# One Trainium2 kernel, last stage: another order of the products, scales on GpSimd, and two last groups without casts

## The reference, cut to what matters

```python
y = y.transpose(0, 2, 1, 3).reshape(Bb, Tt, H * HD)
return y @ Wo
...
def _quant_act(x):
    scale = 127.0 / jnp.clip(jnp.max(jnp.abs(x), axis=-1, keepdims=True), EPS, None)
    xq = jnp.clip(jnp.round(x * scale), -128.0, 127.0) / scale
...
h = jax.nn.gelu(_bitlinear(x, w1), approximate=False)
return _bitlinear(h, w2)
...
x = x + _L0_attn_ref(_layernorm(x, axis=-1), ...)
x = x + _L0_ffn_ref(_layernorm(x, axis=-1), ...)
```

## Time and profile before

| | us |
|---|---|
| median of 3 runs (lowest, highest) | 287.75 (286.58, 287.84) |
| the profiled execution, its own time | 288.18 |
| its span, first to last instruction | 286.3 |
| TensorE busy in the span | 255.1 (89%) |
| VectorE, ScalarE, GpSimd busy | 168.1, 145.3, 130.8 |
| mean granted TensorE clock, of full speed | 0.956 |

### The profile page before, as it was taken

One profiled execution on the slowest core, in us unless ns is written; L12 is line 12 of the kernel. 1 busy time (PEld: TensorE's weight loads), 2 busy tenths in 40 slices (PEclk: granted clock), 3 DMA queues, 4 the chain that ended last, 5 costly groups with the idle time before them and its releaser, 6 DMA issues.

```text
span 286.3 us, 6450 instructions
## 1 busy us (share of the span) xinstructions
PE 255.1 (89%) x2520; PEld 196.6 (69%) x2526; DVE 168.1 (59%) x435; ACT 145.3 (51%) x269; POOL 130.8 (46%) x133
## 2 busy tenths in 40 slices
PE   8577659999999797999999999999989898999663
PEld 7553447777687475777777777777768787888542
DVE  1687656676541345355666555555555769898840
ACT  1231513443444766455555566655543267888662
POOL 0252103230021666197997968585894024332330
PEclk9997977999999799799999999999999999999986
DMA  7999999960193101001010000100000000000001
GB/s 226 346 387 400 359 322 326 379 240 0 13 371 99 37 0 40 0 2 39 0 39 3 14 26 3 38 0 2 2 2 2 0 0 3 19 21 21 25 31 37
DMA packets 18542, 27.74 MB, mean 97 GB/s; under 512 B 1489, under 2 KB 11857, under 8 KB 18513
## 3 DMA queue, kind: packets, MB, share of 16 engines
q1 hardware_dynamic: 17072, 26.35, 27.3%
q10 hardware_dynamic: 1440, 0.99, 1.2%
HBM read 26.28 MB, written 1.05 MB: 95 GB/s over the span
## 4 chain that ended last, share of the span: by engine, by line
PE 71%; DVE 8%; DMA 7%; issue 5%; ACT 5%; SPq 2%; POOL 1%; ACTq 1%; POOLq 0%; DVEq 0%
PE b L1107 15%; PE b L912 12%; PE b L914 10%; PE b L913 10%; PE b L1132 6%; PE b L1120 6%; DMA cl<-in_ctx 4%; DMA bqk<-in_bq 3%; PE b L1005 2%; SPq L171 2%; PE b L1223 2%; PE b L1162 1%; PE b L1213 1%; DVE xn L653 1%; PE b L984 1%
## 5 line engine op out<-in xcount | busy, mean ns | idle before, releaser
L534 ACT ACTIVATE phi<-b 128x512 f32<-128x512 f32 x64 | 34.8, 596 | 45.4 <-PE b L1107 45.4
L354 POOL TENSOR_TENSOR sq_lo<-sq,sq_hi 128x512 fp32r<-128x512 f32 x32 | 40.8, 1283 | 28.8 <-ACT sq_hi L478 28.2
L744 DVE CAST x_hi<-b 128x512 fp32r<-128x512 f32 x32 | 22.1, 692 | 53.6 <-ACT sq_hi L478 53.6
L308 POOL TENSOR_TENSOR lnr<-lnv,mh 128x1 f32<-128x1 f32 x16 | 8.7, 546 | 57.7 <-DVE lnv L627 57.7
L912 PE MATMUL b<-nT_lo,wp_hi 128*128 128x512 f32 x64 | 27.2, 425 | 0.0
L477 ACT ACTIVATE sq<-b 128x512 f32<-128x512 f32 x32 | 19.1, 598 | 14.2 <-PE b L914 14.2
L914 PE MATMUL b<-nT_hi,wp_hi 128*128 128x512 f32 x64 | 25.6, 399 | 0.0
L913 PE MATMUL b<-nT_hi,wp_lo 128*128 128x512 f32 x64 | 25.5, 399 | 0.0
L746 DVE TENSOR_TENSOR x_lo<-b,x_hi 128x512 fp32r<-128x512 f32 x32 | 22.1, 691 | 1.1
L1120 PEld LDWEIGHTS b<-phi,phi 128*64 128x64 f32 x512 | 16.2, 138 | 7.7 <-issue 5.1
L912 PE MATMUL b<-wo_lo,yT_hi 128*128 128x256 f32 x64 | 18.6, 291 | 2.4 <-DVE yT_lo L847 2.4
(11 more groups left out here) (145 smaller groups left out, 644.3 us busy)
## 6 DMA issues: line engine op xcount, KB each, us to landing
cT<-in_ctxT SPq DMA_DIRECT2D x8, 1028.0 KB, 13.9
cn<-in_ctx SPq DMA_DIRECT2D x8, 1024.0 KB, 15.8
wv_raw<-in_aWv SPq DMA_DIRECT2D x1, 1024.0 KB, 15.8
wp_raw<-in_aWq SPq DMA_DIRECT2D x8, 128.0 KB, 2.4
wp_raw<-in_aWk SPq DMA_DIRECT2D x8, 128.0 KB, 3.1
w_raw<-in_w1T SPq DMA_DIRECT2D x1, 1024.0 KB, 4.9
w_raw<-in_w2T SPq DMA_DIRECT2D x1, 1024.0 KB, 7.6
wo<-in_aWo SPq DMA_DIRECT2D x1, 1024.0 KB, 10.1
```

The source lines that it names most:

```text
L354: nc.gpsimd.tensor_tensor(sq_lo[s % 2][t][:], sq[s % 2][t][:], sq_hi[s % 2][t][:].bitcast(F32), ALU.subtract).then_inc(sq_l, 1)
L534: nc.scalar.activation(phi[s % 2][t][a][:], (b2, b3)[a][:], ACT.Exp).then_inc(f_exp, 1)
L744: nc.vector.tensor_copy(x_hi[s % 2][t][:], proj_bank(s, t)).then_inc(x_h, 1)
```

## The change

The halves of y are transposed and copied one by one: TensorE does the first half of group i+1 ahead of the product of group i and the second behind it, and ScalarE and VectorE split their calls to match. The output scales move from `scales` on VectorE to a new output_scale on GpSimd. gelu(i-1) comes in the same step of ScalarE's loop as layer1(i-1), where it came one step later, and quant_h and round_h likewise; a gelu over two elements of a new tile `spare` stands ahead of the stage. The last groups go another way: group 7's first rounding is done by VectorE, its xr3 is transposed as f32 (late_aqTc takes ROUND off in the copy); hidden layers of groups 6 and 7 are transposed as f32 from hr and hr_last, in halves with banks of their own (b0, b1, b4, b5), copied by late_hqTc, and layer 2 of group 6 writes b2. keep_warm(5) issues five matmuls of 128 columns, whose result nobody reads, ahead of them.

```diff
+            def output_scale(k, n, g, ready):
+                pool.wait_ge(ready, g + 1)
+                nc.gpsimd.tensor_tensor(qsc[:, k + 3, g:g + 1], qsc[:, k + 1, g:g + 1], wsum[:, 2 + n:3 + n],
+                                        ALU.mult).then_inc(out_scale[n], 1)
+
+            for i in range(NG + 1):
                 if i < NG:
                     rstd(2, i)
-                    round_a(i)
+                    if i < LAST:
+                        round_a(i)
+                    output_scale(0, 0, i, a_scale)
+                if 0 <= i - 1 < LAST:
+                    round_h(i - 1)
+                if 0 <= i - 1 < NG:
+                    output_scale(4, 1, i - 1, h_scale)
...
-            def yTc(g):
+            def yTc(g, c):
                 if g >= 2:
                     act.wait_ge(o_mm, g - 1)
-                for c in range(2):
-                    act.wait_ge(yT_mm, 2 * g + c + 1)
-                    copy(yT_hi[g % 2][:, 4 * c:4 * c + 4, :], (b0, b1)[c][:]).then_inc(yT_a, 1)
+                act.wait_ge(yT_mm, 2 * g + c + 1)
+                copy(yT_hi[g % 2][:, 4 * c:4 * c + 4, :], (b0, b1)[c][:]).then_inc(yT_a, 1)
...
+            def late_hqTc(g, c):
+                act.wait_ge(hT_mm, 2 * (g - LAST + 1) + c + 1)
+                if g < LAST:
+                    act.wait_ge(f2_mm, g)
+                nc.scalar.activation((hqT, hqT_last)[g - LAST + 1][:, 4 * c:4 * c + 4, :],
+                                     (b0[:], b1[:], b4)[2 * (g - LAST + 1) + c], ACT.Copy, bias=-ROUND
+                                     ).then_inc(hT_a, 1)
+
+            nc.scalar.activation(spare[:], ones[:, 0:2], ACT.Gelu)
+            yTc(0, 0)
+            yTc(0, 1)
             act.wait_ge(s_mask, STEPS)
-            for i in range(NG + 4):
-                if 0 <= i - 2 < NG:
-                    gelu(i - 2)
-                if 0 <= i - 1 < NG:
+            for i in range(NG + 1):
+                if i + 1 < NG:
+                    yTc(i + 1, 0)
+                if 0 <= i - 1 < LAST:
                     cast_a(i - 1)
                     aqTc(i - 1)
-                if 0 <= i - 3 < NG:
+                if 0 <= i - 3 < LAST - 1:
                     hqTc(i - 3)
                 if i + 1 < NG:
-                    yTc(i + 1)
-                if 0 <= i - 2 < NG:
+                    yTc(i + 1, 1)
+                if 0 <= i - 1 < NG:
+                    gelu(i - 1)
+                if 0 <= i - 2 < LAST - 1:
                     cast_h(i - 2)
+            late_hqTc(LAST - 1, 0)
+            late_hqTc(LAST - 1, 1)
+            late_hqTc(LAST, 0)
...
-            def scales(k, n, g, ready):
+            def scales(k, g, ready):
 
                 link(nc.vector.tensor_scalar(qsc[:, k + 1, g:g + 1], qsc[:, k, g:g + 1], Q_EPS, 1.0 / 127.0,
                                              ALU.max, ALU.mult))
                 nc.vector.reciprocal(qsc[:, k + 2, g:g + 1], qsc[:, k + 1, g:g + 1]).then_inc(ready, 1)
-                nc.vector.tensor_scalar(qsc[:, k + 3, g:g + 1], qsc[:, k + 1, g:g + 1], wsum[:, 2 + n:3 + n],
-                                        None, ALU.mult).then_inc(out_scale[n], 1)
...
+                scales(0, g, a_scale)
+                if g == LAST:
+                    dve.wait_ge(a_scale, g + 1)
+                    dve.wait_ge(aq_r, g)
+                    nc.vector.tensor_scalar(xr3[:], xn3[:], qsc[:, 2, g:g + 1], ROUND, ALU.mult,
+                                            ALU.add).then_inc(ar_r, 1)
+
+            def late_aqTc(g):
+                dve.wait_ge(aqT_mm, g + 1)
+                dve.wait_ge(h_mm, 2 * g)
+                nc.vector.tensor_scalar(aqT[:], b3[:, 0:D].rearrange("p (c n) -> p c n", n=P), -ROUND, None,
+                                        ALU.add).then_inc(aqT_cp, 1)
...
+                scales(4, g, h_scale)
+                if g == LAST:
+                    dve.wait_ge(h_scale, g + 1)
+                    for c in range(2):
+                        at = slice(512 * c, 512 * c + 512)
+                        nc.vector.tensor_scalar(hr_last[:, at], hid[g % 2][:, at], qsc[:, 6, g:g + 1], ROUND, ALU.mult,
+                                                ALU.add).then_inc(hr_d, 1)
+
+            def late_hqTc():
+                dve.wait_ge(hT_mm, 4)
+                nc.vector.tensor_scalar(hqT_last[:, HC // 2:HC, :], b5.rearrange("p (c n) -> p c n", n=P), -ROUND, None,
+                                        ALU.add).then_inc(hT_d, 1)
...
-            for i in range(NG + 4):
-                if 0 <= i - 4 < NG:
-                    final(i - 4)
-                if 0 <= i - 2 < NG:
-                    quant_h(i - 2)
-                if i < NG:
-                    x2(i)
-                if i + 1 < NG:
-                    yTc(i + 1)
-                if i < NG:
-                    quant_a(i)
+            for i in range(NG):
+                if i < 3:
+                    yTc(i + 1, 0)
+                x2(i)
+                if i < 3:
+                    yTc(i + 1, 1)
+                elif i < LAST:
+                    yTc(i + 1, 0)
+                quant_a(i)
+                if 3 <= i < LAST:
+                    yTc(i + 1, 1)
+                if i >= 3:
+                    final(i - 3)
+                if i == LAST:
+                    late_aqTc(i)
+                if i >= 1:
+                    quant_h(i - 1)
+            quant_h(LAST)
+            final(LAST - 2)
+            late_hqTc()
+            final(LAST - 1)
+            final(LAST)
...
-            def yTt(g):
+            def yTt(g, c):
                 pe.wait_ge(n_y, 4 * PAIRS - 2 if g < HALF else 4 * PAIRS)
-                for c in range(2):
-                    if g >= 1:
-                        pe.wait_ge(yT_d, 2 * g - 1 + c)
-                    for k in range(4):
-                        mm = pe.transpose((b0, b1)[c][:, k * P:(k + 1) * P], y[:, g, (4 * c + k) * P:(4 * c + k + 1) * P],
-                                          ident[:])
-                    mm.then_inc(yT_mm, 1)
+                if g >= 1:
+                    pe.wait_ge(yT_d, 2 * g - 1 + c)
+                for k in range(4):
+                    mm = pe.transpose((b0, b1)[c][:, k * P:(k + 1) * P], y[:, g, (4 * c + k) * P:(4 * c + k + 1) * P],
+                                      ident[:])
+                mm.then_inc(yT_mm, 1)
...
+            def late_hqTt(g, c):
+                n = g - LAST + 1
+                if n == 0:
+                    pe.wait_ge(hr_r, g + 1)
+                    pe.wait_ge(yT_d, 2 * NG)
+                else:
+                    pe.wait_ge(hr_d, c + 1)
+                    pe.wait_ge(h_act, 2 * NG)
+                for k in range(4):
+                    mm = pe.transpose((b0[:], b1[:], b4, b5)[2 * n + c][:, k * P:(k + 1) * P],
+                                      (hr, hr_last)[n][:, (4 * c + k) * P:(4 * c + k + 1) * P], ident[:])
+                mm.then_inc(hT_mm, 1)
+
             def layer2(g):
-                pe.wait_ge(hqT_cp, g + 1)
                 if g == 0:
                     pe.wait_ge(w_quant, 8)
-                if g >= 1:
-                    pe.wait_ge(fin_r, g)
+                if g < LAST - 1:
+                    pe.wait_ge(hqT_cp, g + 1)
+                    if g >= 1:
+                        pe.wait_ge(fin_r, g)
+                elif g < LAST:
+                    pe.wait_ge(x2_cp, NG)
+                else:
+                    pe.wait_ge(fin_r, g - 1)
                 for c in range(HC):
-                    mm = pe.matmul(b7[:, 0:D], hqT[:, c, :], w2q[:, c, :], start=(c == 0), stop=(c == HC - 1))
+                    if g == LAST - 1 and c % 4 == 0:
+                        pe.wait_ge(hT_a, c // 4 + 1)
+                    if g == LAST and c % 4 == 0:
+                        pe.wait_ge((hT_a, hT_d)[c // 4], (3, 1)[c // 4])
+                    mm = pe.matmul(out_bank(g), (hqT if g < LAST else hqT_last)[:, c, :], w2q[:, c, :], start=(c == 0),
+                                   stop=(c == HC - 1))
                 mm.then_inc(f2_mm, 1)
 
+            def keep_warm(n):
+                pe.wait_ge(hqT_cp, LAST - 1)
+                for _ in range(n):
+                    pe.matmul(b6[:, 0:P], ones[:], ones[:], start=True, stop=True)
+
             pe.wait_ge(f_exp, 8 * PAIRS)
-            for i in range(NG + 4):
+            for i in range(NG + 1):
+                if i + 1 < NG:
+                    yTt(i + 1, 0)
                 if i < NG:
                     project_out(i)
-                if 0 <= i - 1 < NG:
+                else:
+                    hqTt(i - 3)
+                if i >= 1:
                     aqTt(i - 1)
-                if 0 <= i - 3 < NG:
+                if 3 <= i < NG:
                     hqTt(i - 3)
                 if i + 1 < NG:
-                    yTt(i + 1)
-                if 0 <= i - 1 < NG:
+                    yTt(i + 1, 1)
+                if i >= 1:
                     layer1(i - 1)
-                if 0 <= i - 3 < NG:
```

(41 more changed lines are left out.)

17 lines of the change are left out of this document (8 added, 9 removed).

## The result

The changed kernel takes 279.14 us (median of 4, 278.51 to 280.14) against 287.79 of before: ratio 0.971, interval 0.967 to 0.975. Two later comparisons on other chips gave 0.971 (0.967 to 0.974) and 0.971 (0.968 to 0.974). The forecast had the sign and most of the places, but 5.1 us where 8.65 were measured; its range began at 281.0. The profiled execution took 280.14, with a span of 278.3.

The account below looks back on a forecast made before the run. Front limited by filling the pipeline, middle bound by TensorE, tail by latency. Gains of 1.6 (front) and 4.35 (tail), less 0.9 for the clock, gave 5.1 us less and a forecast of 282.6 us; range 281.0 to 284.9.

Parts of the forecast that it names:

- There is no hole to close: a reordering gains nothing here: Middle groups: TensorE's work of 6.15 us a group fills the period of 6.15, so the period stays unchanged.
- the front: Start of the stage: three waits for yT's low half, 2.4 us, go; 0.8 of new waits appear; gain 1.6.
- I expect the low clock again behind it: Tail, after t = 2.7 to 5.4 with 0.7 us of TensorE work: half clock returns, price 0.9 us.
- my first rival: Tail: clock stays up, its gaps being shorter than the earlier one; 0.9 us less, 281.7; chance 0.25.
- The rounding halves: Tail, VectorE's second rounding of group 7: two halves of 512 columns, taken as 0.6 and 0.68 us.
- x: GpSimd's new output-scale multiply, 128x1: taken as 0.32 us by extrapolation, ends 0.1 and 0.55; counts from 0.5 up.
- What lies outside S: Outside the stage: store after final(7) stays 2.6 us; profiled execution 1.9 over its span; median 0.43 lower.
- x = 0.55: Dear GpSimd multiply: under 0.1 us a group plus a later tail, 0.75 in all; loop-bound rival 283.4, chance 0.15.
- x = 2: Very dear GpSimd multiply: last product ends near 275, kernel takes 293 us; slower rival, chance 0.03.
- the wait before aqTt(0): Front, TensorE after product 1: a new wait of about 0.7 us, counted as 0.64, before transposing aq(0).
- the loop of VectorE and GpSimd: Middle: loop from xn to the next rstd takes 5.63 + x against 6.15 us, closing 0.2 inside the period.
- the table load: Ahead of the stage on ScalarE: load 1.30 and small gelu 0.24 end at 220.7, hidden with 0.5 us spare.

Follow-up runs that it names:

- e2: Changed kernel with y transposed whole behind the product, as before the change; ratio to before 0.975 (0.968 to 0.982).
- e12: Changed kernel with both halves of y(i+1) transposed ahead of product i; one run, 285.69 us.
- e7: Kernel before with warming matmuls added in the gaps of its tail; ratio to before 0.999 (0.996 to 1.003).
- e5: Kernel before, unchanged, run again as a control with its own profile; ratio to before 1.000 (0.995 to 1.004).
- e6: Kernel before with only the two-element gelu added ahead of the stage, which moves the table load early; ratio to before 0.993 (0.990 to 0.997).
- e13: Kernel before with only the unused two-column tile added, shifting later addresses by 32 bytes; ratio to before 0.998 (0.994 to 1.001).
- e1: Changed kernel without the special path: groups 6 and 7 go like all others, no warming matmuls; ratio to before 0.984 (0.973 to 0.995).
- e4: Changed kernel without the early two-element gelu, so the table loads in front of gelu(0) again; ratio to before 0.974 (0.967 to 0.981).
- e9: Changed kernel with the output scales back on VectorE; ratio to before 0.970 (0.967 to 0.974).
- e10: Changed kernel again, unaltered; ratio to before 0.971 (0.967 to 0.974).
- e14: Changed kernel whose early gelu writes unused columns of an old tile, so no addresses shift; 278.66 us, ratio to before 0.974 (0.971 to 0.977).
- e15: Changed kernel a third time, unaltered; 277.92 us, ratio to before 0.971 (0.968 to 0.974).
- e3: Changed kernel without the five warming matmuls; ratio to before 0.971 (0.964 to 0.978).
- e8: Changed kernel without warming, with aqTt(7) ahead of hqTt(5) and quant_h(7) reduced behind each half of gelu(7); ratio to before 0.974 (0.967 to 0.980).
- e11: Changed kernel with the same three tail edits as e8, run again; 277.68 us, ratio to before 0.970 (0.966 to 0.974).

## Why the prediction was wrong

The forecast median was 282.6 and 279.14 was measured, 3.5 us less. S accounts for 2.0 of them: 0.74 in P, and 1.27 in the tail, of which 0.85 is the clock and 0.42 the size of the rounding halves. The other 1.5 lie outside S.

**"There is no hole to close: a reordering gains nothing here"** is a step that failed. P came out 0.74 shorter than predicted. The waits that I foresaw are there (0.62 before aq(0) for a forecast of 0.64), so the front is right by its own terms. But I took the work of a group as fixed because TensorE was busy all the time, and the time for the same work depends on its order too. A full group of the middle took 6.06 in the mean instead of 6.15, and e2 gives it back. Counted in the same way, with the waits taken out, the two groups of the front gained about 0.1 each. Over six groups that is about 0.5 of the 0.74, by an estimate from these periods; about 0.1 more is that aqTt(0) came sooner than walked, and where the rest lies is open. In the rows most of the saving lies where transposes are followed by the product and not by layer 1 (0.08, see e12), and 0.04 in layer 2, which issues in 0.87 instead of 0.91. Why that is so stays open.

**"I expect the low clock again behind it"** is the step that cost most in S, 0.85. The stretch came out as walked (transposes of 0.7 us in 2.6 us, 265.99 to 268.6), and the granted clock stayed at 1.00. This was my first rival, with 0.25. Its price was not tested in the changed kernel, where the clock never fell; in the old one it was 0.80 (e7). The forecast that the warming matmuls would take 2.2 us at half clock fell with it; they took 1.1 at full clock and did nothing. The tails on record:

| tail | waits of TensorE in order, us | granted clock |
|---|---|---|
| before (e5 and e6 likewise) | 2.21, then 1.12, 1.78, 1.12 | 0.50 from 271.4 to 274.8 and from 281.6 on |
| e13 | 2.21, 0.26, 0.40, 1.45, then 1.59, 1.12 | 1.00 up to 274.0, then 0.50 to the end |
| e1 | 1.75, 0.26, 1.05, 1.12, then 1.12 | 1.00 up to 270.4, then 0.50 up to 273.8 |
| after (e2, e4, e9, e10, e12, e14, e15 alike) | 1.05, 0.75, 0.33 | 1.00 |
| e3 | 1.05, 0.75, 0.82, 0.41 | 1.00 |
| e8 (e11 nearly alike) | 1.11, 0.64, 0.24 | 1.00 |
| e7, with warming matmuls | 0.42, 0.39, 1.45, 0.17 | 1.00 |

The tails with the special path kept the clock in all eleven profiles. But no rule comes out of the table: a wait of 2.21 brought it down in before and did not in e13, and 1.75 did not in e1 where 1.05 and 1.12 did. What decides it stays open.

**The rounding halves were mis-sized** by 0.4. They take 0.91 together, not 1.28. x, the multiply on GpSimd, was mis-sized too: it is 0.19 long and the next instruction starts 0.15 after it, not 0.32, so that the extrapolation from 256 and 512 columns does not hold at one. But that is not in the result. The walk beside the trace, in us after the end of the last product:

| | forecast | measured |
|---|---|---|
| xn(7) starts | 2.5 | 2.29 |
| xr3(7) is rounded | 4.27 | 3.96 |
| transposes of hq(5) start | 4.03 | 3.95 |
| both gelus of group 7 are done | 7.3 | 7.30 |
| quant_h(7) is done | 8.95 | 8.95 |
| second rounding half is done | 10.35 | 9.89 |
| layer 2 of group 7 starts | 11.7 | 11.35 |
| final(7) starts, clock up | 12.85 | 12.43 |

xn came 0.2 sooner, and that was lost again at TensorE, which still waited for hq(5). Only the rounding halves moved the end.

**What lies outside S**, 1.5 us, I had taken as unchanged. In the profiled pair 0.90 lie ahead of S. Whether the new tile has a part in it is open; the numerators started at 217.71 to 220.65 in three profiles of the changed kernel and at 219.92 and 221.55 in two of the kernel before. Some of the 8.65 may be luck of these runs: the later comparisons gave 8.3 and 8.0.

Two side sums of the prediction do not follow from its own terms. At x = 0.55 its loop is 6.18 against 6.15, 0.03 a group, which makes about 0.4 with the tail and not 0.75; at x = 2 its rule puts the end of the last product near 272.4 and the kernel at 291.7, not at 275 and 293. Neither enters the forecast.

Right were the wait before aqTt(0), the loop of VectorE and GpSimd, which never became the bound (VectorE waits 1.5 us in all for the reciprocal root, 0.8 of it in the tail), and the table load: it is hidden, and the copy of yT waits for TensorE. The row decided this rightly; the spare gelu starts at 219.59, 1.29 after the load began.

The Trainium skill (ScalarE: Activation LUTs, "What ACT_TABLE_LOAD costs") counts a drain of about 1.38 us on top of the load; this trace does not show it.

What each part is worth, by the run that takes it away:

| part | P | tail |
|---|---|---|
| special path, with the clock that it keeps (e1) | 0 | 2.84 |
| halves (e2) | 1.82 | 0 |
| early load (e4) | 0.76 | 0 |
| scales on GpSimd (e9) | 0.31 | 0 |
| warming (e3) | 0 | 0 |
| sum of these | 2.89 | 2.84 |
| whole change | 2.33 | 4.76 |

In P the parts overlap, since their sum is more than the whole. In the tail 1.9 us are left over. I put them down to gelu, quant_h and round_h a step sooner, which no run took away by itself: that is argued, not shown.

## What to carry to other kernels

Measure a changed stage from a fixed event ahead of it to its end, not only the kernel: S repeated to 0.1 us where the whole time spread over 1 to 4. An engine that is busy without a gap still has a period that depends on the order of its work, here by 0.1 us in 6. Moving one buffer's wait from behind a long operation to ahead of it can decide over 7 us (e12). In a pipeline's tail count latencies, and give the last items their own path. Read the granted clock of the tail in more than one profile, since the same queues had it low in different places (before, e13), and try without warming before adding it.

## What the runs showed of the hardware

- A 128x1 two-input multiply on GpSimd takes 0.19 us, a 128x1 power 0.54; 256 and 512 columns (0.80, 1.28) would have said 0.32.
- Rounding 512 columns from SBUF on VectorE took 0.49 us (0.91 for two, one behind the other), a subtraction of the same width from a bank 0.69.
- Four f32 transposes in a row are issued in 0.36 us ahead of the product with Wo and in 0.44 ahead of layer 1 (bf16); eight in 0.79 and 0.88.
- The same queues, with the same wait of 2.21 us of TensorE, had the granted clock at 0.50 at its end in one profile (before) and at 1.00 for more than five us behind it in another (e13).
- A table load took 1.28 us, and the two-element gelu of 0.20 us behind it started 1.29 us after the load had begun.
